# Scatter of messages by plain fp32 products in place of a rounded part and a remainder

## The reference

```
h = ssp(f_ij @ W1 + b1)
Wij = (h @ W2 + b2) * rcut_ij[:, None]
s, v = hs[idx_j], hv[idx_j]                  # gather of node channels
edge = concatenate([t_s1 * Wf0, t_s2 * Wf1, t_v1 * Wf2, t_v2 * Wf3, ...])
agg = segment_sum(edge, idx_i, num_segments=n)   # scatter
s_in = concat(agg0, agg1); v_in = concat(agg2:5, agg5:8)
os2 = ssp(s_in @ w_f2o1_s / sqrt(2F)) @ w_f2o2_s / sqrt(B)
ov2 = (v_in @ w_f2o1_v) @ w_f2o2_v, scaled
```

## Time and profile before

| | us |
|---|---|
| median of 3 runs | 76.31 |
| lowest, highest | 76.28, 79.52 |
| profiled execution, its time | 76.64 |
| its span, first to last instruction | 74.8 |
| PE busy | 67.6 |
| DVE busy | 58.8 |
| ACT busy | 36.9 |
| POOL busy | 29.1 |

### The profile page before, as it was taken

The page is one execution under the profiler, slowest core; times in us unless marked ns, Lnnn a source line. Parts: engine busy times, 40 slices in busy tenths (PEclk is TensorE's granted clock), DMA queues, the critical chain, the costliest instruction groups (busy, mean ns, idle before and its releaser), DMA issues.

```text
span 74.8 us, 1309 instructions
## 1 busy us (share of the span) xinstructions
PE 67.6 (90%) x475; PEld 55.4 (74%) x475; DVE 58.8 (79%) x135; ACT 36.9 (49%) x62; POOL 29.1 (39%) x35
## 2 busy tenths in 40 slices
PE   3996989999999879899999999999999999999630
PEld 1242466488643448799999999999999999998520
DVE  4657999999395999999399999949495959982570
ACT  0600389400922876938434457757737484822600
POOL 4000000007986500191009797791938585600000
PEclk9999999999999999999999999999999999999999
DMA  0899999870000000000000000000000000000035
GB/s 6 175 367 252 394 476 437 347 247 12 0 0 0 0 0 0 0 4 0 0 9 0 0 0 0 0 0 0 13 0 0 0 0 0 0 0 0 9 112 169
DMA packets 3050, 5.66 MB, mean 76 GB/s; under 512 B 540, under 2 KB 1936, under 8 KB 2916
## 3 DMA queue, kind: packets, MB, share of 16 engines
q1 hardware_dynamic: 2274, 5.14, 19.6%
q10 hardware_dynamic: 770, 0.44, 2.1%
HBM read 5.06 MB, written 0.52 MB: 75 GB/s over the span
## 4 chain that ended last, share of the span: by engine, by line
PE 65%; DVE 11%; DMA 8%; ACT 5%; issue 5%; SPq 1%; POOL 1%
PE bank L644 21%; PE bank L628 20%; PE bank L512 8%; DMA f_sb<-f_t 8%; PE bank L560 4%; PE bank L538 4%; PE bank L520 3%; PE bank L605 2%; PE bank L557 2%; DVE hW_lo L412 2%; DVE hX L409 2%; DVE x L419 1%; ACT za L196 1%; ACT h L233 1%; ACT za L240 1%
## 5 line engine op out<-in xcount | busy, mean ns | idle before, releaser
L644 PE MATMUL bank<-OsR,Mh 128*128 128x256 f32 x68 | 16.8, 287 | 0.0
L644 PE MATMUL bank<-OsR,Ml 128*128 128x256 f32 x68 | 16.5, 284 | 0.0
L628 PE MATMUL bank<-H,OdT 128*128 128x128 f32 x136 | 16.5, 275 | 0.0
L628 PEld LDWEIGHTS bank<-H,OdT 128*128 128x128 f32 x136 | 15.9, 192 | 0.0
L335 POOL TENSOR_TENSOR Ml<-dst_bc,Mh 128x512 fp32r<-128x512 f32 x8 | 10.3, 1286 | 12.2 <-ACT Mh L267 12.2
L644 PEld LDWEIGHTS bank<-OsR,Ml 128*128 128x128 f32 x68 | 12.9, 190 | 0.0
L644 PEld LDWEIGHTS bank<-OsR,Mh 128*128 128x128 f32 x68 | 12.8, 188 | 0.0
L512 PEld LDWEIGHTS bank<-OdT,Os 128*128 128x128 bf16 x68 | 7.0, 105 | 3.6 <-DVE OdT L350 1.3
L512 PE MATMUL bank<-OdT,Os 128*128 128x256 bf16 x68 | 9.4, 298 | 0.1
L267 ACT ACTIVATE Mh<-dst_bc 128x512 fp32r<-128x512 f32 (+1 forms) x9 | 5.5, 607 | 7.9 <-DVE dst_bc L464 7.9
L339 POOL TENSOR_TENSOR Ml<-dst_bc,Mh 128x512 fp32r<-128x512 f32 x7 | 9.0, 1292 | 0.0
(11 more groups left out here) (109 smaller groups left out, 111.4 us busy)
## 6 DMA issues: line engine op xcount, KB each, us to landing
dst_bc<-dst_row SPq DMA_DIRECT2D x1, 2176.0 KB, 13.2
w_sb<-w SPq DMA_DIRECT2D x1, 1024.0 KB, 8.4
x_sb<-x SPq DMA_DIRECT2D x1, 512.0 KB, 4.8
out<-x_sb SPq DMA_DIRECT2D x2, 192.0 KB, 1.9
f_sb<-f_t SPq DMA_DIRECT2D x1, 378.0 KB
b_sb<-bias SPq DMA_DIRECT2D x1, 256.0 KB, 13.3
w_sb<-w ACTq DMA_DIRECT2D x1, 128.0 KB, 4.3
out<-x_sb ACTq DMA_DIRECT2D x1, 128.0 KB, 1.9
```

The lines of the kernel that those rows point to most:

```text
L628: last = nc.tensor.matmul(gbank[g % RG][:, j * C:(j + 1) * C], OdT[:, a, t * P:(t + 1) * P], H[:, a, :], start=(a == 0), stop=(a == NH - 1))
L644: last = nc.tensor.matmul(bank[4 + b][:, 0:N], part[:, g % RG, j, feats(b)], OsR[:, g % RG, j, :], start=(t == 0 and part is Mh), stop=(t ...
```

## The change

The rings Mh and Ml and everything that fills them go. OsR becomes plain fp32. The scatter takes the messages M themselves as the stationary operand, in one product per tile and half, and waits for svw and MA. Since M is now read by the scatter, VectorE waits for scatter g-3 before it writes group g's messages, where it waited for the remainder of group g-3.

```diff
-        OsR = sb("OsR", [P, RG, TG, N], fp32r)
+        OsR = sb("OsR", [P, RG, TG, N])
...
-        Mh = sb("Mh", [P, RG, TG, S * F], fp32r)
-        Ml = sb("Ml", [P, RG, TG, S * F], fp32r)
...
             for g in range(NG):
-                n = tiles(g)
-                o = g % RG
-                act.wait_ge(q["svw"], g + 1)
-                if g >= RG:
-                    act.wait_ge(q["scat"], g - RG + 1)
-                nc.scalar.activation(Mh[:, o, 0:n, feats(1)], M[:, o, 0:n, feats(1)], ACT.Copy).then_inc(q["MhB"], 1)
-                act.wait_ge(q["MA"], g + 1)
-                nc.scalar.activation(Mh[:, o, 0:n, feats(0)], M[:, o, 0:n, feats(0)], ACT.Copy).then_inc(q["MhA"], 1)
                 if g + 5 < NG:
                     filters_out(g + 5)
...
-            for g in range(LATE):
...
-                nc.gpsimd.tensor_tensor(Ml[:, o, 0:n, feats(1)], M[:, o, 0:n, feats(1)], Mh[:, o, 0:n, feats(1)].bitcast(fp32),
-                                        ALU.subtract).then_inc(q["MlB"], 1)
...
                 if g >= RG:
-                    dve.wait_ge(q["MlA"], g - RG + 1)
+                    dve.wait_ge(q["scat"], g - RG + 1)
...
-            for g, b, rounded, left in ((LATE - 1, 0, "MhA", "MlA_late"), (LATE, 0, "MhA", "MlA_late"),
-                                        (LATE, 1, "MhB", "MlB_late")):
...
             def scatter(g):
                 pe.wait_ge(q["OsR"], g + 1)
+                pe.wait_ge(q["svw"], g + 1)
                 for b in (1, 0) if g < LATE else (0, 1):
-                    if g == LATE:
-                        pe.wait_ge(q[("MlA_late", "MlB_late")[b]], 2 - b)
-                    elif (g, b) == (LATE - 1, 0):
-                        pe.wait_ge(q["MlA_late"], 1)
-                    else:
-                        pe.wait_ge(q[("MlA", "MlB")[b]], g + 1)
+                    if b == 0:
+                        pe.wait_ge(q["MA"], g + 1)
                     for j in range(tiles(g)):
                         t = TG * g + j
-                        for part in (Mh, Ml):
-                            last = nc.tensor.matmul(bank[4 + b][:, 0:N], part[:, g % RG, j, feats(b)], OsR[:, g % RG, j, :],
-                                                    start=(t == 0 and part is Mh), stop=(t == T - 1 and part is Ml))
+                        last = nc.tensor.matmul(bank[4 + b][:, 0:N], M[:, g % RG, j, feats(b)], OsR[:, g % RG, j, :],
+                                                start=(t == 0), stop=(t == T - 1))
```

More of the change, by code:

```diff
@@ L141, in gnn_preln_kernel @@
                  "y WY OdT OsR "
-                 "G m0 vys sw2 vyv svw red MA MhA MhB MlA MlB MlA_late MlB_late scat "
+                 "G m0 vys sw2 vyv svw red MA scat "
                  "scatA aggA aggT wc wcs o1 os1 ta te tl rl os1T fin os2 ov o")
```

## The result

The changed kernel took 92.27 us in the median of four executions (91.56 to 93.28), the kernel before 76.53 us; the ratio is 1.204, with a 95% interval of 1.193 to 1.215. The forecast was 89.4 us, 88.3 to 90.8. The sign and most of the size are right, and 1.5 us are missing even to the upper end. An execution of either kernel may lose TensorE's full clock for part of its first 14 us, and by their mean granted clock (0.955 to 0.969) all four of these had lost it.

A forecast was written before the change was run, and what follows sets the result against it. TensorE was taken to bound the kernel, its stream a plain sum from 41.6 to 68.6 us. 13.3 - 0.2 = 13.1 us on a 74.8 us span gave 87.9, against the median 89.4 us; range 88.3 to 90.8.

The forecast's parts named there:

- (a): Scatter on TensorE: 136 fp32r instructions become 136 plain fp32 ones, 217 ns each instead of 119.4; 13.3 us more.
- Rival 3: Scatter: the fp32r instruction's excess over 107 ns comes with every pass, so plain takes 238.8 ns; 92.3 us, chance 0.05.
- (b): Scatter weight loads: 136 remain, hidden under instructions of 217 ns; nothing.
- (c): Rounding copies on ScalarE and subtractions on GpSimd and VectorE go; none is in the chain, so nothing gained.
- (d): The scatter's waits now name the messages themselves; these are ready early enough that TensorE is never kept waiting.
- (e): VectorE's new wait for scatter g-3 before writing a message buffer, from group 3 on; nothing.
- (f): End of the scatter: TensorE's idle 0.21 us before L662 vanishes; -0.2 us.
- the cover: At the end, L484 just covers final products reaching VectorE about 0.2 us later; up to 0.2 us if it fails.
- Rivals 1 and 2: Scatter: 112 ns per instruction from weight load, 75.3 us, chance 0.03; or one instruction of one pass, 70.6 us, chance 0.02.
- sustained pace: Scatter at the page's 98 ns per instruction, 13.3 us in all, would gain 2.9 us: 73.4 us; chance 0.01.

The follow-up runs named there:

- fifth run: The changed kernel run again, unaltered; median 89.71 us of six executions, four at 89.36 to 89.81 and two at 92.83 and 93.05.
- experiment 2: The kernel before with five extra matmuls on zeros in TensorE's first waits; median 76.84 us, with one of twelve executions at 89.79.
- experiment 5: The changed kernel run again, unaltered; median 89.71 us of six executions, the four at the full clock 1.170 to 1 against the kernel before.
- experiment 1: The changed kernel with five extra matmuls on zeros in TensorE's first waits; median 90.16 us, ratio 1.179 to the kernel before.
- experiment 8: The changed kernel without its 6 warm-up matmuls; 93.14 us in four executions.
- experiment 3: The kernel before without its 6 warm-up matmuls; two of twelve executions at 76.4 and 77.0 us, nine between 78.6 and 81.6, one at 136.89.
- experiment 4: The kernel before with five extra early matmuls on zeros and plain fp32 scatter products for half 1 of the channels alone; 83.19 us.
- experiment 6: The changed kernel with five extra early matmuls on zeros, scatter messages and one-hots in fp32r, remainder left out; 71.25 us, ratio 0.930.

## Why the prediction was right in its sum and wrong in its number

**(a) The scatter's price.** 217 ns were taken and 13.3 us summed; 216 ns were measured, in every block and in three kernels, and 13.0 us between the same two points of the timeline, the vanished idle time included. The two passes per instruction, read off L538 at 512 columns, hold at 256. The gather's 112 ns would have misled by 8 ns. Rival 3 (238.8 ns, 92.3 us) gives the measured time almost to the digit and is nevertheless false: its blocks would take 3.8 us and they take 3.45.

**(b), (c), (d), (e).** All nothing, as put. In the fifth run's profile the chain doesn't leave TensorE between the first gather and L629, VectorE's wait for gathers is 14.1 us (14 forecast), and GpSimd's last work ends at 34.0 us. That what left ScalarE and GpSimd, and the new wait of the ring, cost or gain nothing was read from the profile and not tried apart from the rest.

**(f) The end.** The 0.21 us vanished: L629 follows the last scatter instruction at once. L455 ends at 83.48 on the chain and L461 follows on it, so the cover held.

**The rivals.** Rivals 1 and 2 fall with 216 ns and 136 instructions. The Trainium skill's sustained pace (page "TensorE: Matmul & The Clock Gate", section "Back-to-back issue gap"), some 98 ns at 256 columns if read as a line between the page's two figures, an estimate from the page, is under all measured: 109.5 for bf16, 119 for fp32r, 216 for plain fp32.

**The step that failed** is the first sentence of the sum: "13.3 - 0.2 = 13.1 us on a span of 74.8, so 87.9 us". It takes for granted that everything ahead of 41.6 us stays as it is in one profiled execution. The table of times already had the contrary in it: the third execution of the kernel before took 79.52 us, 3.2 more than its neighbours, and the prediction allowed 0.5 us for the spread. What the runs showed in its place: in the result's profile the scatter began 2.45 us late, behind products at a granted clock of 0.50 (L491 at 3.97 us in place of 2.21), and an execution of either kernel loses some 3.2 to 3.4 us in this way (experiments 2 and 5; in four executions of the kernel before only 1.6 to 2 us). It happened to 17 of 39 executions of the kernel before and to 6 of 10 of the changed one, the four of the result among them. The table of times alone would have given the prediction a second case, 89.4 + 3.2 = 92.6 us with a chance of about one in three, and its range would have reached there. What the change itself does to the time, 13.0 to 13.3 us, was forecast to 0.3 us, and the span of 87.9 us came out in the fifth run's profile, by the mechanism that was summed and not by luck.

**What stays open.** Whether the changed kernel loses the clock more often than the kernel before (6 of 10 against 17 of 39 doesn't tell), and what decides it. Two profiles of the same start show a difference; TensorE's timeline of the result's execution and of the fifth run's:

```profile
3.74 0.72 PE L483 MATMUL bank<-OdT,Os 128*128 128x256 bf16 x4
4.94 1.05 PE L483 MATMUL bank<-OdT,Os 128*128 128x256 bf16 x8 [0.48 <-DVE OdT L327]
7.13 3.97 PE L491 MATMUL bank<-f_sb,w_sb 84*128 84x512 f32 x6 [1.14 <-DMA f_sb<-f_t]
```

```profile
3.78 1.04 PE L483 MATMUL bank<-OdT,Os 128*128 128x256 bf16 x4
4.98 1.10 PE L483 MATMUL bank<-OdT,Os 128*128 128x256 bf16 x8 [0.17 <-DVE OdT L327]
7.64 2.21 PE L491 MATMUL bank<-f_sb,w_sb 84*128 84x512 f32 x6 [1.56 <-DMA f_sb<-f_t]
```

Where the clock was lost, the first four adjacency matmuls were already at the full one (0.72 us), then TensorE idled 0.48 and 1.14 us, and the clock fell. Where it wasn't lost, they were still slow (1.04 us), in a stretch where TensorE waits for data anyway, and the clock rose in time for the products that count. Idle time alone doesn't decide, since the second has more of it (1.73 us against 1.62). The filled kernel of experiment 1 had the early rise too (0.76 us) and didn't fall. That the fall comes from an early rise followed by idle time is what two profiles suggest, and isn't shown; experiment 8 lost its time without an early rise.

A second difference goes with the loss as well. In the five profiles without filling, the products of f_sb start at 7.13 us (the result) and 7.26 us (experiment 8) where time was lost, and at 7.62, 7.64 and 7.74 us (the kernel before, experiments 5 and 3) where it wasn't. An early arrival of f_t, or something that goes with it, is thus a rival that no run here separates. With the filling it does no harm: those products start at 7.25 and 7.16 us in experiments 4 and 6 and take 2.10 and 2.21 us.

## What to carry to other kernels

Count the instructions that the page gives per product of the code, and read the pace of one at the widest shape at hand: a plain fp32 product cost four passes of its columns, a pair of fp32r products two and some overhead, so splitting fp32 into two rounded parts pays here as long as the rounding lies beside TensorE. One rounded part in place of two took the loop from TensorE to VectorE (71.25 us), and two parts in bf16 reusing one-hots that are there anyway was a little faster than the kernel before too (75.75 us). Both keep fewer bits of a message, and what that does to the accuracy of the result wasn't measured here. And look at the single times of a kernel before summing on its profile: where one of three is 4% off, the clock's early loss is a case with a price and a chance of its own. A few matmuls on zeros in TensorE's first waits removed it here in all but one of 28 executions; what they buy is steadier times, since the median of all executions of the kernel before is no higher without them (76.97 and 76.82 us in two series against 76.84).

## What the runs showed that I hadn't expected

The clock row of the page reads nine in the first three slices of every profile here, and the stretch of the warm-up matmuls of the kernel before is given as 1.00, while six of 512 columns take 2.54 us, 423 ns each, which is the 1.2 GHz level:

```profile
1.18:3.72 2.54, 2.54 (x6) 0.73 (x6) 1.00 0.65 131
```

At the full clock the same shape takes about half: the first two filling matmuls span 0.59 us in experiment 1, where the clock had risen, and 1.06 us in the profile of experiment 2. Experiment 8 shows it at a greater price: its clock row reads nine in all slices but the last, and the six instructions of L491 take 4.21 us, where 2.21 us is their time at the full clock. So the granted clock is not to be believed ahead of its first change, and matmuls of a known shape are the better clock. The executions without warm-up show the same in their means: 0.986 to 1.0 with 2 to 5 us lost.

The fp32r instruction of 256 columns takes 119 ns where the bf16 one takes 109.5 (1.91 and 1.75 us for 16), while plain fp32 at 216 ns is within 2% of its bare two passes (213.3 ns).
